# SP's order of issues in a two-stage depthwise convolution: X's halo at the head of the next period, and loads and stores of a pair of units in one piece

## What is computed

```
x = x + L0(gn(x))   # L0(v) = a0*v + a1*dw1x1(v) + a2*dw3x3(v) + a3*dw5x5(v), depthwise, weights by channel
x = x + L1(gn(x))   # L1(v) = one 3x3 filter and a bias, the same for all channels
```

## Time and profile before

| what | value |
|---|---|
| median of 3 runs | 428.78 us (428.14 to 429.96) |
| the profiled execution's own time | 432.64 us |
| its span, first to last instruction | 430.8 us |
| busy: PE, DVE, ACT, POOL | 318.5, 318.1, 304.1, 262.3 us |
| mean granted clock of PE | 0.903 |
| moved by DMA | 69.40 MB, mean 161 GB/s |

### The profile page before, as it was taken

How to read it: one execution, slowest core, us unless ns; L and a number is a source line. 1 busy time by engine, 2 the same in 40 slices (tenths; PEclk the granted TensorE clock), 3 DMA queues, 4 the chain that set the end, 5 groups by cost and what they waited for, 6 DMA issues and landing times.

```text
span 430.8 us, 12547 instructions
## 1 busy us (share of the span) xinstructions
PE 318.5 (74%) x5206; PEld 276.8 (64%) x5206; DVE 318.1 (74%) x688; ACT 304.1 (71%) x372; POOL 262.3 (61%) x206
## 2 busy tenths in 40 slices
PE   2491586754986998679894998499848989898440
PEld 2361273643986798459883897389836989897220
DVE  7861899971886998399929994889649996779620
ACT  1407257089999699939995899759993999977320
POOL 6405055058788578827885588738882788865601
PEclk9997596995999899969996999889998999999685
DMA  6689488201687769676986788676868514731965
GB/s 151 169 174 204 129 188 169 73 3 41 159 200 164 199 177 210 158 189 202 199 194 171 198 184 202 161 214 173 189 163 223 145 41 118 201 97 28 264 173 146
DMA packets 112829, 69.40 MB, mean 161 GB/s; under 512 B 4540, under 2 KB 109892, under 8 KB 112772
## 3 DMA queue, kind: packets, MB, share of 16 engines
q1 hardware_dynamic: 106088, 65.31, 60.5%
q10 hardware_dynamic: 6684, 3.29, 3.3%
HBM read 41.10 MB, written 27.48 MB: 159 GB/s over the span
## 4 chain that ended last, share of the span: by engine, by line
DVE 33%; DMA 21%; SPq 13%; ACT 13%; PE 9%; issue 4%; ACTq 2%; POOL 2%; POOLq 0%; DVEq 0%
DVE xt L697 15%; DVE stats L641 13%; DMA xt<-in_x_dram 10%; PE ps L377 8%; DMA edge_scratch<-gnX 6%; ACT gn_f L551 5%; SPq L236 5%; ACT gnX L552 4%; ACT cross L561 3%; SPq L216 3%; DMA edge_scratch<-gnY 2%; SPq L250 2%; POOL gnX L864 1%; SPq L263 1%; ACTq L244 1%
## 5 line engine op out<-in xcount | busy, mean ns | idle before, releaser
L377 PE MATMUL ps<-gnX,band 64*64 64x512 f16 x2880 | 181.6, 397 | 29.9 <-DVE xt L697 18.1
L377 PEld LDWEIGHTS ps<-gnX,band 64*64 64x64 f16 x2880 | 161.1, 188 | 46.6 <-issue 40.2
L697 DVE SCALAR_TENSOR_TENSOR xt<-ps,unscale,xt 128x512 f32<-128x512 f32 (+1 forms) x194 | 143.8, 747 | 22.9 <-PE ps L377 20.1
L641 DVE BATCH_NORM_STATS2 stats<-xt 128x6 f32<-128x384 f32 x256 | 120.9, 546 | 45.6 <-DMA xt<-in_x_dram 44.9
L377 PE MATMUL ps<-gnY,band 64*64 64x512 f16 x1728 | 116.8, 414 | 33.7 <-DVE xt L697 33.7
L864 POOL TENSOR_TENSOR gnX<-gn_f,gnX 128x768 f16<-128x768 f32 x60 | 92.7, 1545 | 60.7 <-ACT gnX L552 60.7
L377 PEld LDWEIGHTS ps<-gnY,band 64*64 64x64 f16 x1728 | 97.9, 190 | 49.1 <-ACT gnY L552 23.0
L551 ACT ACTIVATE gn_f<-xt,g_add,g_mul 128x768 f32<-128x768 f32 x120 | 122.1, 1017 | 4.9 <-DVE g_add L681 4.3
L864 POOL TENSOR_TENSOR gnY<-gn_f,gnY 128x768 f16<-128x768 f32 x60 | 92.7, 1545 | 31.0 <-ACT gnY L552 31.0
L561 ACT ACTIVATE cross<-ps,unscale 64x512 f32<-64x512 f32 x94 | 64.2, 683 | 51.0 <-PE ps L377 49.4
L873 POOL TENSOR_TENSOR xt<-xt,cross 128x512 f32<-128x512 f32 x47 | 61.7, 1315 | 57.3 <-ACT cross L561 57.2
(11 more groups left out here) (78 smaller groups left out, 97.9 us busy)
## 6 DMA issues: line engine op xcount, KB each, us to landing
out_dram<-xt SPq DMA_DIRECT2D x56, 384.0 KB, 4.8
xt<-in_x_dram SPq DMA_DIRECT2D x48, 384.0 KB, 6.4
band<-diag_scratch SPq DMA_DIRECT2D x48, 160.0 KB, 3.0
haloX<-edge_scratch SPq DMA_DIRECT2D x32, 123.4 KB
xt<-in_x_dram SPq DMA_DIRECT2D x20, 192.0 KB, 4.3
xt<-in_x_dram ACTq DMA_DIRECT2D x12, 192.0 KB, 6.0
out_dram<-xt SPq DMA_DIRECT2D x12, 192.0 KB, 4.0
haloX<-edge_scratch SPq DMA_DIRECT2D x32, 61.7 KB
```

What stands on the lines that cost most here:

```text
L377: mm = nc.tensor.matmul(ps[to, c, half, :], weights(rows, half), moving(rows, half), start=first, stop=last)
L641: st = nc.vector.bn_stats(stats[:, q_of(at, i) % 2, at, b, e, :], flat[:, SUB * e:SUB * (e + 1)])
L697: ev = nc.vector.scalar_tensor_tensor(out=here, in0=ps[frm, c, half, :].rearrange("h (b w) -> h b w", b=NB), scalar=unscale[rows, at:at + ...
```

## The change

The order of SP's issues is changed, nothing else. X's way in of unit j + 1 moves from period j, between the DMAs of images 2 and 3, to the head of period j + 1. In odd periods the loads of images 0 and 1 come right behind Y's way out, ahead of the bands, and those of images 2 and 3 behind Y's way in, so that all eight stand ahead of X's way out. In even periods the stores of images 0 and 1 stay ahead of X's way out, and images 2 and 3 follow behind it without X's way in between them.

```diff
--- before.py
+++ after.py
@@ -345,21 +345,24 @@
 
             for j in range(PERIODS):
                 y = j - LAG
+                loading = j % 2 == 1 and j < PERIODS - 1
+                if 1 <= j < NU:
+                    edges_in(sp, X, j)
                 if 0 <= y < LAST:
                     edges_out(sp, Y, y)
+                if loading:
+                    in_and_out(j, (0, 1))
                 if 1 <= j < LAST:
                     load_band(j + 1)
                 if j % 2 == 0 and 2 <= j < NU - 2:
                     save_pair(j // 2 + 1, k_out)
                 if 0 <= y < LAST:
                     edges_in(sp, Y, y)
-                in_and_out(j, (0, 1))
+                in_and_out(j, (2, 3) if loading else (0, 1))
                 if j + 1 < NU:
                     edges_out(sp, X, j + 1)
-                in_and_out(j, (2,))
-                if j + 1 < NU:
-                    edges_in(sp, X, j + 1)
-                in_and_out(j, (3,))
+                if not loading:
+                    in_and_out(j, (2, 3))
             unit_ready(LAST)
             for b in (0, 1):
                 store_unit(sp, LAST, b)
```

## The result

The changed kernel took 451.02 us (median of 4 runs, 449.42 to 452.61) against 429.37 us for the kernel before (4 runs, 428.14 to 430.62). The ratio is 1.0504, with a 95% interval of 1.0453 to 1.0555: slower by 21.6 us where 2.5 were forecast. The profiled execution took 449.42 us on a span of 447.6, so by the profiles the change costs 449.42 - 432.64 = 16.8 us. The 16.8 is what the traces can explain. A ratio with an interval is taken here over the executions within 1.5% of the fastest of the same kernel, a median over all of them.

What follows compares the result with a forecast made beforehand. SP's own loop of issues and border-row landings bounds the kernel; the loop stays near 46 us. Unit 13's 0.8 plus the tail's 1.7 make 2.5 us, on the median 428.78 giving 431.3, range 424 to 437.

Steps and rivals of the forecast that it cites:

- The mechanism: DVE's 34.7 us stall for loads goes and returns as PE's wait for halo rows, with SP closing the loop.
- the forecast of the loop: From one store group to the next: 16.7 + 29.6 = 46.3 us against 46.1, nothing gained.
- 19.3 us from the first load to X's way in: In loading periods, X's border rows land behind eight loads and the bands, so transfers decide: 19.3 us, 4.2 later.
- From the way in to the stores: In loading periods, one load group and the wait for Y's border rows leave: 13.1 us becomes 10.3.
- The half with stores: In even periods, all stores precede X's way in: taken as 16.7 us against 17.9.
- First store and tail: First store at 137.35 against 135.84, 1.5 us late; the tail, through unit 15's halo, 1.7 us late.
- Unit 15's halo: In the tail, two more stores ahead make it 2.4 us late, quicker landing returns 0.7: 1.7, bounds 0.5 and 2.9.
- Bands later, more than a unit before use: nothing: Bands are issued about 3 us later, more than a unit before use, at no cost.
- The signature: Profile after: DVE's load wait near zero, X's way in 19 us after first load, PE halo waits, loop near 46.
- The prefetch pays: Faster rival: border rows don't wait for all eight loads, or loads drain faster; 414, middle case 425.3; chance 0.27.
- The queue gets slower: Slower rival: upper bounds hold, loop 48.0, from stores delaying loads or halo rows holding bulk; 439, middle 435; chance 0.23.
- The stall only shrinks: Rival: SP reaches the loads late, DVE keeps a wait of 1 to 3 us; same 431; no separate chance.

Runs made afterwards that it cites:

- e9: Changed kernel with all eight loads of a loading period in one piece behind the bands and Y's way in; 454.81 us, ratio 1.0586.
- e12: Changed kernel with Y's way in of a loading period behind the last load, bands still between the load groups; 462.1 us against 429.97 before.
- e5: Changed kernel with loads of pairs 4 to 7 carrying half their bytes, same number of issues; 427.94 us against 430.56 before.
- e1: Changed kernel with the new order in loading periods only, even periods as before; 451.52 us, ratio 1.0464 to the kernel before.
- e2: Kernel before with only X's way in for odd units moved behind all stores, to the next period's head; 434.17 us, ratio 1.008.
- e3: Kernel before with X's way in at the head of the next period everywhere, loads and stores left in place; 434.8 us, ratio 1.0023.
- e8: As e3, but six loads instead of four ahead of X's way out in a loading period; 441.87 us, ratio unsettled, 1.006 to 1.029.
- e7: Kernel before with X's way out, from unit 3 on, issued by ACT in place of SP; 439.29 us, ratio 1.023.
- e10: Kernel before with two loads instead of four ahead of X's way out in a loading period; 440.85 us, ratio 1.0231.

## Why the prediction was wrong, point by point

**The mechanism was right, the sizes weren't.** DVE's stall gone (0.8 us), its place taken by PE's wait for halo X (38.3 us in 11 places, 5.6 at most), rows landing behind the eighth load and not before: all as forecast. So was the reading that SP closes the loop: over the four loops SP waited 16.8 us for X's rows and only 3.7 us for a compute engine, DVE, before stores. What was wrong most was the forecast of the loop, 46.3 us: it is 49.9. Four times 3.6 is 14.4, which is the miss by the profiles (16.8 measured less 2.5 forecast, 14.3).

**The step that failed: 19.3 us from the first load to X's way in.** It was 21.4. The prediction built it of 4.6 for the first load, 11.8 for the seven others, 2.1 for the bands "at the loads' pace", and 0.8. Counted to the landing of the eighth load, e9, with nothing among the loads, measured 16.7 us for the forecast's 4.6 + 11.8 = 16.4, so pace and landing were sized well. With the bands among the loads (e12) it was 19.2: the bands cost 2.5 us for 2.1. With Y's way in there too (the changed kernel) it was 20.7: another 1.5, for which the sum has no term at all. The rows came 0.7 behind the eighth load for 0.8. So of the 2.1 us that are missing 1.5 are Y's way in between the two load groups, 0.4 the bands and 0.3 the loads. The split rests on one execution of e12, though on four loops of it.

The slip behind it shows in the prediction's own words. The prediction compared 13.5 us of SP's issues with 19.3 of transfers and concluded that the transfers decide. But the stream has a break in the middle, and there SP's time counts: it reached the fifth load 9.65 us after the first (154.70 to 164.35), where the rows of before gave 7.8 (3.2 + 1.9 + 2.7). The first four took it 3.98 us and the bands 2.78, in place of 3.22 and 1.86. With the forecast's own 4.6 from issue to landing the fifth load could not land before 14.25; the forecast had it at 4.6 + 5.04 + 3.78 = 13.4. It landed at 169.91, 15.2 after the first issue. The DMA engines' work has a hole at that place in three of four loops and none in e12, so SP's late arrival cost time there; how much the transfer of Y's rows adds to it isn't separated. The order of landing is not strict either: the first band, issued behind the fourth load, landed at 164.78, ahead of that load's 165.27.

**From the way in to the stores: 10.3 forecast, 10.7 found.** The removed load group and the removed wait for Y's rows did leave. 0.4 off.

**The half with stores: 16.7 forecast, 17.8 found.** This half wasn't shortened. Before, its mean is 17.3, and the 17.9 of the earlier trace rows against which I set 16.7 was its longer kind. X's way in behind eight stores took 4.0 to 4.6 us to issue, 4.2 in the mean, where I took 3.75 less 0.3. That is about 0.8 of the 1.1 us a loop: a row from behind six stores was carried over to a place behind eight, with a deduction.

Together 2.1 + 0.4 + 1.1 = 3.6 per loop.

**First store and tail.** The first store came at 136.39, 1.0 earlier than the 137.35 forecast. Unit 13 followed its store group 0.5 later than worked out, and the tail cost 2.2 for 1.7. With 14.4 these sum to 14.4, the miss by the profiles to a tenth. That the tail comes so near is luck. Unit 15's halo alone was forecast at 1.7 us and cost 4.3: its way in came 12.6 us after its group's first store (9.5 before), 3.0 more where 2.4 were taken, and from there to the matmul it took 7.7 us, where a quicker landing had been given as 6.3. The 2.1 us that came back in the last unit's Y rows were in no sum.

**Bands later, more than a unit before use: nothing.** No wait for the bands appears among the larger ones. Y's halo, said to be covered by X's, wasn't quite: 10.0 us in 5 places.

**The signature.** The loop is above the 47.5 that the prediction named as the sign of being wrong. X's way in was 19 us forecast, 21.4 found; the rest of the signature held. One remark of the prediction counts wrong without harm: a pair of units has two ways out and in of each kind, not three.

**The rivals.** *The prefetch pays* fell: e5 shows that the rows wait for the loads' bytes, and in after they landed with the eighth load. The advice of the Trainium skill, page "DMA: Bandwidth & Descriptors", section "Rules for kernel authors", to issue early and wait late, was right of the loads' own waiter and wrong of the total here, as weighed; this trace has 38.3 us of PE's waits in the place of DVE's 34.7. *The queue gets slower* named the direction and one of the mechanisms ("halo rows hold up the bulk behind them"), but its upper bounds, 48.0 a loop, lay below the measured 49.9. The bound of the stretch before X's way in was the fault: it had no upper end beyond 19.3, although the bands share their place with four halo transfers and with SP's issues for them. With 21.4 as its upper end this case would have come to 439 + 4 x 2.1, about 447, still short of 451.02. *The stall only shrinks* didn't come up.

**What the loss consists of.** By e1 and e2 it lies mostly in the loading period: 1.0464 for that part of the change alone, with a wait for stores that the whole change doesn't have, and 1.008 for the other part alone. In the changed kernel's own loops the half with loads grew by 3.3 us and the half with stores by 0.5. By the dose series it lies in the number of loads ahead of X's way out. By e5 it is their transfer time, and by e9 and e12 what stands among them. By the windows, that time isn't won back later, since behind the way in the DMA engines run at 103 GB/s where before they ran at 164.

**Left open.** Whether the DMA engines, at a share of 0.89 in the first stretch where loads alone read 1.1 to 1.3, could have carried the bands faster in pieces of another size wasn't tried. PE's granted clock was 0.84 in both stretches of after and 1.00 in those of before; PE had waited for halo rows there. How much of the loss comes through this clock wasn't separated. Within the four loops, which hold 15.0 of the 16.8 us, it can hardly be much: SP, which closes the loop, waited there only 3.7 us for a compute engine, in the list of waits for 136.39 to 335.91:

```profile
SPq L263 <- DVE xt L700: 3.7, 6, 0.9
```

PE's busy time grew by 8 us in all, of which only what lies on the chain counts.

## What to carry to other kernels

When one queue carries both bulk loads and a small round trip on which the next unit depends, the bulk in front of the round trip is paid nearly in full (from e3 over e8 to e9 2.9 to 3.0 us for each two loads, whose transfers take 3.4), and bulk behind it can be carried while the issuer waits: look for the split at which both waits are small, and price a reordering by the bytes ahead of the small transfer and by the breaks in the stream of large ones while the issuer is busy with small ones. Time the stretch between the first bulk issue and the dependent landing as a whole from the row nearest to it, counting every transfer that stands in it, small ones too. A stall in the list of waits is worth what the loop that contains it gives back, not its own length.

## What the runs showed that I had not expected

- Small rows issued by ACT did not pass four loads issued by SP: issued at 162.51 in e7, landed at 170.21, between the fourth (169.10) and the fifth load (171.06). The Trainium skill, page "DMA: Bandwidth & Descriptors", section "Queues, rings and completion order", says that each DMA engine takes turns between the queues it has work for, packet by packet; by that the border rows from ACT's own queue would have landed ahead of the four, which this trace doesn't show.
- A hole of 2.64 us in SP's issues of large transfers, with four loads still out, left the DMA engines short of work: their share read 0.58, 0.98, 0.26 and 0.52 over two microseconds in the four loops, where loads in one piece keep it at 1.1 to 1.3.
- SP's issues slow down behind many large transfers: eight loads took 10.53 us to issue in e9, 1.32 each, where two at a time took 1.37 in e10, 0.69 each. Which limit holds them, the runs don't show.
- The same eight loads, taken at one stretch, land nearly at the pace of 1.68 us measured from four in the earlier trace rows: 1.73 us each in the mean of four loops of e9, and 17.1 us to X's way in for 17.2 worked out.
